# Row maxima of two neighbouring PSUM banks in one VectorE operation, in a transformer kernel with four rotating banks

## The chip, the cores and the metric

The kernel runs on one core of one Trainium2 chip. A core has five engines that run side by side and meet at semaphores: TensorE (PE; its weight loads are a row of their own, PEld), VectorE (DVE), ScalarE (ACT), GpSimd (POOL) and SyncE (SP), which here issues DMAs. The metric is the device time of one launch in microseconds (us). The kernel before takes 1293.03 us, the median of 3 runs (1291.48 to 1293.97).

## What is computed

Two sequences of 1024 tokens with 512 channels go through four residual stages. The first one, causal attention with 32 query heads of 16 channels over a single key/value head and an ALiBi slope per head, is the one that the change touches:

```python
x = x + _layernorm(_L0_attn_ref(_layernorm(x), Wqkv, Wo))      # the stage of the change
x = x + _layernorm(_L0_ffn_ref(_layernorm(x), ...))            # 4-bit weights, 512 -> 1376 -> 512
x = x + _layernorm(_L1_attn_ref(_layernorm(x), ...))           # a masked linear layer
x = x + _layernorm(_L1_ffn_ref(_layernorm(x), ...))            # a linear layer with a Fourier update

# in _L0_attn_ref
scores = jnp.einsum('bqhd,bkd->bhqk', q, k) * scale
scores = jnp.where(causal, scores + slopes * (pos_k - pos_q), NEG_INF)
probs = jax.nn.softmax(scores, axis=-1)
attn = jnp.einsum('bhqk,bkd->bqhd', probs, v).reshape(B, S, H)
return attn @ Wo
```

## The kernel before

Attention goes by 16 blocks of 128 queries (`BLOCKS`: the eight of sequence 0 in rising order, the eight of sequence 1 in falling order). A block is gone through twice.

First pass, `p1` in the code: TensorE computes scores with the queries on the partitions, only to find the maximum of each row. The keys of a block are cut into segments of 512, 256 or 128 (`segments`). One unit ("p1", i, z, h) fills one PSUM bank of 512 columns: one head by 512 keys, two by 256 or four by 128, with a mask matmul added where the segment holds the diagonal (`row_max` in `tensor`, lines 1314 and 1317). VectorE then takes the maxima of that bank with one TENSOR_REDUCE of 512 elements per partition into `mx` (`row_max` in `vector`, line 1125). All blocks together have 576 such banks. When a block has its last unit, `mx` is joined over the segments, turned on TensorE ("mt", line 1364), split into three bf16 parts and sent by DMA into three rows of the block's stacked queries `QS` (line 853).

Second pass: TensorE computes the scores again, now with keys on the partitions and the maximum already subtracted through those rows ("tile", line 1393; mask at 1395) into the three banks of `ST`; ScalarE takes the exponential (line 1048); four tiles make a quad, and TensorE multiplies it with the values ("pv", line 1407, eight records a quad) into the bank `PO`. There are 576 tiles and 144 quads. After a block its sums are turned ("ot", line 1369), divided by the row sums on VectorE (lines 1173 and 1174), turned again ("at", line 1373, split at 1185) and multiplied by Wo ("wo", lines 1379 to 1381).

PSUM has eight banks: three of `ST`, one of `PO` and four of `bank`, the ring (`RING = 4`). Every use of the ring takes the next bank, `AT[u] % RING`: the 576 units of the first pass and 147 other uses (by kind: 32 ot, 20 xt, 20 q, 16 mt, 16 at, 16 wo, 6 dv, 6 ds, 5 kv, 5 vt, 5 dt). TensorE waits before a use until the use four places earlier has been read (`bank_for`), which VectorE or ScalarE tells after reading it.

Every engine runs a fixed program. The order of the work is written by `plan_order`, a list scheduler in Python that runs when the kernel is built. It has a cost for each kind of work (`took` for TensorE; the dictionary in `commit` for the others) and takes in turn what is ready, by a due time. In it a first-pass unit costs TensorE 218 ns plus its mask, and VectorE 690 ns. A unit competes for TensorE with a due time of VectorE's load less 400 ns, tiles with ScalarE's load, other uses of the ring with now plus 500 or 600 ns, and pv with now plus 1500 ns.

Of the kernel before, what the change touches and what calls it, by code (L numbers as in the profile page):

```python
# [15 lines left out]
ALU = mybir.AluOpType  # L16
# [8 lines left out]
P = 128  # L25
# [155 lines left out]

def maxima_of(i):

    return [("p1", i, z, h) for z, (_, w, _) in enumerate(segments(BLOCKS[i][1])) for h in range(0, NH, 512 // w)]


QUAD0 = [0]
# [30 lines left out]
def plan_order():  # L218
# [1 line left out]

    took = {"dt": 400, "dv": 520, "ds": 300, "p1": 218, "tile": 218, "pv": 1060, "xt": 400, "q": 700, "kv": 700, "vt": 400, "mt": 200, "ot": 400, "at": 400, "wo": 700}
    reads = {"pe": 280, "act": 270, "dve": 270, "pool": 200, "sp": 0}
    free = {"pe": 0, "act": 0, "dve": 0, "pool": 0, "sp": 0}
    end, order = {}, {e: [] for e in free}
# [9 lines left out]
    def known(*keys):  # L236
        t = 0
        for k in keys:
            if k not in end:
                return None  # L240
            t = max(t, end[k])
        return t
# [1 line left out]
    def latest(*ts):  # L244
        return None if None in ts else max(ts)

    def bank_ready():
        n = len(bank_of) - RING
        return known(("bank", bank_of[n])) if n >= 0 else 0

    def open_piece(k):
        for t in range(PIECES[k][2]):
# [30 lines left out]

    def pe_choices():
        out = []
        dve_load = free["dve"] + sum(690 for j, r in pend["dve"] if r <= free["pe"] + 300)
        act_load = free["act"] + sum(600 for j, r in pend["act"] if r <= free["pe"] + 300)
        if at["p1"] < len(p1):
            u = p1[at["p1"]]
            i = u[1]  # L290
            deps = [("stacked", i), ("ks", keys_piece(i))]
            if u == maxima_of(i)[0] and i >= 2:
                deps.append(("pe", ("mt", i - 2)))
            out.append((latest(known(*deps), bank_ready()), dve_load - 400, u))
        if at["tile"] < 4 * QUADS:
            n = at["tile"]
            i = BLOCK_OF[n // 4]
            t = known(("max", i), *([("exp", n - ST_RING)] if n >= ST_RING else []))
            out.append((t, act_load, ("tile", n)))
        if at["pv"] < QUADS:  # L300
            q = at["pv"]
            i, a, kb = quad_place(q)
            deps = [("exp", 4 * q + j) for j in range(4)] + [("v", keys_piece(i))]
            if kb == 0 and q:
                deps.append(("evac", q - 1))
            out.append((known(*deps), free["pe"] + 1500, ("pv", q)))
        if turn:
            out.append((latest(end[turn[0][1]], bank_ready()), 0, turn[0][0]))
        for work, late in ((finish_work, 600), (chunk_work, 500)):
            if work:  # L310
                u, need = work[0]
                t = known(need)
                if u[0] not in STEPPED or u[-1] == 0:
                    t = latest(t, bank_ready())
                out.append((t, free["pe"] + late, u))
        return [x for x in out if x[0] is not None]

    def commit_pe(t, u):
        kind = u[0]
        ms = took[kind]  # L320
        if kind == "p1":
            _, w, diag = segments(BLOCKS[u[1]][1])[u[2]]
            ms += 216 * P // w if diag else 0
        if kind == "tile" and diagonal(u[1] // 4):
            ms += 216
        if kind in ("q", "kv") and PIECES[u[1]][2] < 3:
            ms = 720
        e = t + ms
        log.append((t, e, "pe", u))
        end["pe", u] = e  # L330
        free["pe"] = e
        order["pe"].append(u)
        name = u[:-1] if kind in STEPPED else u
        if kind not in ("tile", "pv") and (kind not in STEPPED or u[-1] == 0):
            bank_of.append(name)
        ready = e + reads["pe"]
        if kind == "p1":
            at["p1"] += 1
            pend["dve"].append((u, ready))
            for i, k in ((1, 2), (4, 3), (6, 4), (AFTER_AT, AFTER)):  # L340
                if u == maxima_of(i)[-1]:
                    open_piece(k)
            if u == maxima_of(AFTER_AT)[0]:
                sp_issue(("load", AFTER), e)
                pend["pool"].append((("clear",), e))
                for k in range(CODE_RING):
                    sp_issue(("codes", k), e)
        elif kind == "tile":
            at["tile"] += 1
            pend["act"].append((("exp", u[1]), ready))  # L350
            i = BLOCK_OF[u[1] // 4]
            if u[1] + 1 == TILE_ENDS[i + 1]:
                end["tiles", i] = e
        elif kind == "pv":
            at["pv"] += 1
            end["pv", u[1]] = e
            i, a, kb = quad_place(u[1])
            if kb == BLOCKS[i][1]:
                pend["act"].append((("evac", i, a), ready))
        else:  # L360
            for work in (finish_work, chunk_work, turn):
                if work and work[0][0] == u:
                    work.pop(0)
            if kind in ("xt", "mt", "at", "dt") or (kind in STEPPED and u[-1] == 1):
                pend["act"].append((name, ready))
            if kind in ("vt", "ot"):
                pend["dve"].append((u, ready))
            if kind == "dv":
                pend["act"].append((u, ready))
            if kind == "ds":  # L370
                end["full", u] = ready
                if codes_after(u[1]) is not None:
                    k = codes_after(u[1])
                    sp_issue(("codes", k), max(e, end["q4", k - 2]))
                    pend["dve"].append((("codes", k), max(e, end["codes", k])))
            if kind == "q" and u[-1] == 1:
                sp_issue(("qout", u[1], u[2]), e + 3800)
            if kind == "xt" and u[1] and u[1] + 1 < NC and u[2] == PIECES[u[1]][2] - 1:
                sp_issue(("load", u[1] + 1), e + 2000)
            if kind == "mt":  # L380
                sp_issue(("mdma", u[1]), e + 2300)
                if u[1] + AHEAD < NB:
                    stacks_due.append(u[1] + AHEAD)
        try_stacks()
# [30 lines left out]
    def commit(e, t, j):  # L415
# [38 lines left out]
                pend["dve"].append((j, f + 100))  # L454
        elif e == "dve":
            f = t + {"mx": 200, "mt": 280, "ot": 700, "stats": 900, "mt3": 280, "ys": 1150, "vt": 300, "kv": 750, "norm": 2300, "index": 900, "onehot": 1200,
                     "zeros": 2700, "scales": 1650, "codes": 2600}.get(kind, 690)
            done = f + reads["dve"]
            if kind in ("p1", "xt", "q", "kv", "vt", "mt", "ot", "at", "ds"):
                end["bank", j] = done  # L460
# [113 lines left out]
def uses_in_order():  # L574

    begun, ended = list(FIRST), list(FIRST)
    for u in ORDER["pe"]:
        if u[0] in STEPPED:
            (begun if u[-1] == 0 else ended).append(u[:-1])
        elif u[0] not in ("tile", "pv"):  # L580
            begun.append(u)
            ended.append(u)
    return begun, ended


BEGUN, ENDED = uses_in_order()
AT = {u: n for n, u in enumerate(BEGUN)}
FULL = {u: n + 1 for n, u in enumerate(ENDED)}


# [84 lines left out]
def attention(nc, sem, half_neg, x_dram, wqkv, wo, ident_d, identb_d, mask_d, pos_d, krows_d, gmask_d, x1_dram, ident, identb,  # L675
              wx, xT, xin, QP, qrest, mats, table_loads, dq):
    with ExitStack() as ctx:
# [97 lines left out]
        def at(u):  # L775
            return bank[:, AT[u] % RING, :]

        def full(eng, u):

            eng.wait_ge(bank_full, FULL[u])  # L780
# [23 lines left out]
        def banks_freed(eng, which):  # L804

            for r in which:
                freed(eng, [u for u in BEGUN if AT[u] % RING == r][-1])

        def scores_read(eng):
            eng.wait_ge(p_done, 4 * QUADS)  # L810
# [279 lines left out]
        def vector(v):  # L1090
# [29 lines left out]
            def row_max(u):  # L1120
                _, i, z, h = u
                _, w, _ = segments(BLOCKS[i][1])[z]
                m = 512 // w
                full(v, u)
                v.tensor_reduce(mx[:, i % 2, z, h:h + m], at(u).rearrange("p (m k) -> p m k", m=m), AX.X, ALU.max).then_inc(bank_free_dve, 1)  # L1125

            def join_max(i):
                zs, k = len(segments(BLOCKS[i][1])), i % 2
# [167 lines left out]
        def tensor(pe):  # L1296
            pe.wait_ge(consts_in, 32)

            def bank_for(u):

                if AT[u] >= RING:
                    freed(pe, BEGUN[AT[u] - RING])

            def row_max(u):
                _, i, z, h = u
# [5 lines left out]
                    pe.wait_ge(ks_ready, keys_piece(i) + 1)  # L1311
                bank_for(u)
                for j in range(m):
                    last = pe.matmul(at(u)[:, j * w:(j + 1) * w], QS[0:ROWS1, slot, h + j, :], KS[b][0:ROWS1, k0:k0 + w],  # L1314
                                     start=(j == 0 or not diag), stop=(not diag or w > P), skip_group_check=True)
                if diag:
                    last = pe.matmul(at(u).rearrange("p (m k) -> p m k", m=m)[:, :, w - P:w], identb[:, :],  # L1317
                                     mask[:, 0, 0:m * P].rearrange("p (m k) -> p m k", m=m), start=False, stop=True, skip_group_check=True)
                last.then_inc(bank_full, 1)

            def fill(u, step=None):
# [1001 lines left out]
```

## Time and profile before

| | us |
|---|---|
| median of 3 runs | 1293.03 |
| lowest, highest | 1291.48, 1293.97 |
| the profiled execution | 1289.91 |
| its span, first to last instruction | 1288.1 |
| first pass: first and last row maximum start at | 39.1, 637.9 |
| mean granted TensorE clock | 0.977 of full speed |

The profile is of a single execution. "Busy" is the time that an engine has an instruction in work; matmuls overlap one another, so that a TensorE that is busy need not be at its peak. A wait is told as the idle time of an engine ahead of an instruction, with the instruction that ended it. Since weight loads run under the matmul in front, a wait of PEld need not stop the array, and one of PE does. Some matmul records can be missing from a trace.

### The profile page before, as it was taken

What the parts mean: (1) busy time and instruction counts of PE and PEld (TensorE: products, weight loads), DVE (VectorE), ACT (ScalarE), POOL (GpSimd) and SP (SyncE); (2) the same over time, 40 slices, a digit from 0 to 9 for tenths busy, and PEclk for the clock granted to TensorE, in tenths of its full rate; (3) what the DMA queues carried; (4) which work ended last, traced back from release to release, by engine and by line L of the source; (5) the groups of instructions that cost most, each with busy time, mean ns of one, the idle gap of its engine ahead of it and who ended that gap; (6) DMA issues with size and microseconds to landing.
All of it is one profiled execution on the core that took longest, in us unless ns stands there. A gap on an engine that the chain in (4) does not pass through costs nothing. (4 is left out here: it accounts for less than half of the span.)

```text
span 1288.1 us, 16700 instructions
## 1 busy us (share of the span) xinstructions
PE 1170.8 (91%) x6137; PEld 715.2 (56%) x6208; DVE 715.8 (56%) x1374; ACT 583.2 (45%) x1047; POOL 338.5 (26%) x366
## 2 busy tenths in 40 slices
PE   4879999999989999999998799999999999299995
PEld 4535534543543433344535577788788787256663
DVE  4378598688678897788713643331421300655654
ACT  5425456465547677857574443211111111134443
POOL 1214114112220231211034554111211111115554
PEclk9989999999989999999999999999999999699998
DMA  4451502400140420303120222300200100500304
GB/s 157 97 83 55 94 18 42 108 17 18 29 87 1 107 34 18 75 18 67 28 99 26 73 66 87 107 22 1 98 1 1 66 1 1 150 28 5 126 0 130
DMA packets 71567, 72.15 MB, mean 56 GB/s; under 512 B 39826, under 2 KB 45226, under 8 KB 71468
## 3 DMA queue, kind: packets, MB, share of 16 engines
q1 hardware_dynamic: 67284, 60.35, 18.8%
q0 software_dynamic: 3152, 8.63, 2.1%
q10 hardware_dynamic: 1056, 2.16, 0.5%
q8 instruction: 47, 0.77, 0.2%
q14 instruction: 28, 0.23, 0.1%
HBM read 51.86 MB, written 18.87 MB: 55 GB/s over the span
## 5 line engine op out<-in xcount | busy, mean ns | idle before, releaser
L1125 DVE TENSOR_REDUCE mx<-bank 128x1 f32<-128x512 f32 (+2 forms) x576 | 364.6, 684 | 98.5 <-PE bank L1317 54.7
L1048 ACT ACTIVATE PT<-ST 128x512 f32<-128x512 f32 x576 | 311.4, 600 | 106.4 <-PE ST L1393 62.4
L1314 PE MATMUL bank<-KS,QS 125*128 125x512 bf16 (+2 forms) x896 | 204.1, 309 | 12.5 <-DMA QS<-q_scratch 4.2
L1393 PE MATMUL ST<-QS,KS 128*128 128x512 bf16 x527 | 185.0, 383 | 9.1 <-DMA QS<-mparts 3.3
L1407 PE MATMUL PO<-PT,V 128*32 128x512 f32 x1152 | 152.8, 604 | 1.4 <-ACT PT L1048 1.0
L1694 DVE TENSOR_TENSOR f_h<-f_h,f_pair 128x512 f32<-128x512 f32 (+1 forms) x44 | 30.2, 687 | 207.5 <-ACT f_h L1643 207.5
L1314 PEld LDWEIGHTS bank<-KS,QS 125*128 125x128 bf16 x896 | 78.5, 99 | 113.3 <-DVE mx L1125 33.5
L56 PE MATMUL f_pair<-f_xT,gw 128*128 128x512 f32 (+1 forms) x352 | 140.0, 398 | 0.0
L58 PE MATMUL f_pair<-f_xT,gw 128*128 128x512 f32 (+1 forms) x352 | 137.9, 392 | 0.0
L57 PE MATMUL f_pair<-f_xT,gw 128*128 128x512 f32 (+1 forms) x352 | 137.9, 392 | 0.0
L1643 ACT ACTIVATE f_h<-f_pair 128x512 f32<-128x512 f32 (+1 forms) x44 | 26.3, 598 | 218.9 <-PE f_pair L58 218.8
L1393 PEld LDWEIGHTS ST<-QS,KS 128*128 128x128 bf16 x576 | 51.5, 97 | 125.2 <-ACT PT L1048 76.2
L1607 POOL TENSOR_TENSOR f_h_part<-f_h,f_h_part 128x512 fp32r<-128x512 f32 (+1 forms) x44 | 56.9, 1294 | 228.6 <-ACT f_h_part L1647 228.6
L905 POOL TENSOR_TENSOR yrstd<-ymom,half_neg 128x1 f32<-128x1 f32 x16 | 9.0, 562 | 358.8 <-DVE ymom L1202 358.8
L58 PEld LDWEIGHTS f_pair<-f_xT,gw 128*128 128x128 f32 (+1 forms) x352 | 65.7, 187 | 15.3
L56 PEld LDWEIGHTS f_pair<-f_xT,gw 128*128 128x128 f32 (+1 forms) x352 | 65.6, 186 | 15.0 <-ACT y L1026 0.3
L57 PEld LDWEIGHTS f_pair<-f_xT,gw 128*128 128x128 f32 (+1 forms) x352 | 65.6, 186 | 14.4
L1761 PE MATMUL f_Y<-dw,f_h_part 128*128 128x512 f32 (+1 forms) x176 | 71.3, 405 | 2.1 <-POOL f_h_part L1607 2.1
L1763 PE MATMUL f_Y<-dw,f_h_part 128*128 128x512 f32 (+1 forms) x176 | 68.7, 390 | 0.0
L1762 PE MATMUL f_Y<-dw,f_h_part 128*128 128x512 f32 (+1 forms) x176 | 68.6, 390 | 0.0
L1317 PE MATMUL bank<-mask,identb 128*128 128x128 bf16 (+2 forms) x246 | 67.1, 273 | 0.0
L2150 PE MATMUL l_psum<-l_wT,l_xT 128*128 128x512 f32 x128 | 54.2, 423 | 0.0
(208 smaller groups left out, 1806.6 us busy)
## 6 DMA issues: line engine op xcount, KB each, us to landing
QS<-q_scratch SPq DMA_DIRECT2D x96, 128.0 KB
l_x<-x_dram SPq DMA_DIRECT2D x12, 512.0 KB, 4.1
q_scratch<-QP SPq DMA_DIRECT2D x36, 128.0 KB, 1.9
xres<-_attn_hidden_states_dram POOLq DMA_DIRECT2D x16, 256.0 KB, 3.1
x_dram<-xout POOLq DMA_DIRECT2D x16, 256.0 KB, 2.4
xin<-x_dram SPq DMA_DIRECT2D x4, 1024.0 KB, 7.6
f_xsum<-x_dram SPq DMA_DIRECT2D x4, 1024.0 KB, 7.2
x_dram<-f_xsum SPq DMA_DIRECT2D x4, 1024.0 KB, 4.6
```

The lines of the kernel that those rows point to most:

```text
L56: pe.matmul(out, w_hi(c), x_hi(c), start=(c == 0), stop=False)
L57: pe.matmul(out, w_hi(c), x_lo(c), start=False, stop=False)
L58: last = pe.matmul(out, w_lo(c), x_hi(c), start=False, stop=(c == chunks - 1))
L1048: act.activation(PT[:, quad % PT_RING, n % 4, :], ST[:, n % ST_RING, :], ACT.Exp).then_inc(p_done, 1)
L1125: v.tensor_reduce(mx[:, i % 2, z, h:h + m], at(u).rearrange("p (m k) -> p m k", m=m), AX.X, ALU.max).then_inc(bank_free_dve, 1)
L1314: last = pe.matmul(at(u)[:, j * w:(j + 1) * w], QS[0:ROWS1, slot, h + j, :], KS[b][0:ROWS1, k0:k0 + w], start=(j == 0 or not diag), stop=( ...
L1317: last = pe.matmul(at(u).rearrange("p (m k) -> p m k", m=m)[:, :, w - P:w], identb[:, :], mask[:, 0, 0:m * P].rearrange("p (m k) -> p m k" ...
L1393: last = pe.matmul(dst, KS[b][0:ROWS2, kb * P:(kb + 1) * P], QS[0:ROWS2, slot, h:h + 4, :], start=True, stop=not diag)
L1407: last = pe.matmul(PO[32 * j:32 * (j + 1), :], V[b][:, kb, :], PT[:, q % PT_RING, j, :], start=(kb == 0), stop=(kb == qb))
L1761: pe.matmul(Y[:, t, :], hi(h_parts[0][0:w, s, at]), hi(dw[0:w, 0, n % 2, :]), start=(n == 0), stop=False)
L1762: pe.matmul(Y[:, t, :], hi(h_parts[0][0:w, s, at]), hi(dw[0:w, 1, n % 2, :]), start=False, stop=False)
L1763: last = pe.matmul(Y[:, t, :], hi(h_parts[1][0:w, s, at]), hi(dw[0:w, 0, n % 2, :]), start=False, stop=(n == NT - 1))
```

## The change

A unit of the first pass becomes two neighbouring banks: heads h.. in the first and heads 16 + h.. in the second. TensorE fills both (each matmul and mask is issued for t = 0 and 1), signals once, and VectorE reads both with one TENSOR_REDUCE of 1024 elements per partition. There are 288 units instead of 576. The ring still has four banks, and a pair may start at bank 0, 1 or 2; where it would start at bank 3, that bank is left out once (`skipped`, `take_banks`). A pair waits until both of its banks are free. In the planner a pair costs TensorE 436 ns plus two masks and VectorE 1130 ns.

```diff
 def maxima_of(i):
-    return [("p1", i, z, h) for z, (_, w, _) in enumerate(segments(BLOCKS[i][1])) for h in range(0, NH, 512 // w)]
+    return [("p1", i, z, h) for z, (_, w, _) in enumerate(segments(BLOCKS[i][1])) for h in range(0, NH // 2, 512 // w)]
+
+def banks_of(u):
+    return 2 if u[0] == "p1" else 1
+
+def skipped(n, count):
+    return int(count == 2 and n % RING == RING - 1)
+
+def take_banks(taken, u):
+    if skipped(len(taken), banks_of(u)):
+        taken.append(taken[len(taken) - RING])
+    taken.extend([u] * banks_of(u))
...
-    took = {"dt": 400, "dv": 520, "ds": 300, "p1": 218, "tile": 218, "pv": 1060, ...
+    took = {"dt": 400, "dv": 520, "ds": 300, "p1": 436, "tile": 218, "pv": 1060, ...
...
-    def bank_ready():
-        n = len(bank_of) - RING
-        return known(("bank", bank_of[n])) if n >= 0 else 0
+    def bank_ready(count=1):
+        n = len(bank_of) - RING + skipped(len(bank_of), count)
+        return known(*(("bank", bank_of[x]) for x in range(n, n + count) if x >= 0))
...
-        dve_load = free["dve"] + sum(690 for j, r in pend["dve"] if r <= free["pe"] + 300)
+        dve_load = free["dve"] + sum(1130 if j[0] == "p1" else 690 for j, r in pend["dve"] if r <= free["pe"] + 300)
...
-                     "zeros": 2700, "scales": 1650, "codes": 2600}.get(kind, 690)
+                     "zeros": 2700, "scales": 1650, "codes": 2600, "p1": 1130}.get(kind, 690)
...
+        def both(u):
+            return bank[:, AT[u] % RING:AT[u] % RING + 2, :]
...
             def row_max(u):      # VectorE
                 full(v, u)
-                v.tensor_reduce(mx[:, i % 2, z, h:h + m], at(u).rearrange("p (m k) -> p m k", m=m), AX.X, ALU.max).then_inc(bank_free_dve, 1)
+                v.tensor_reduce(mx[:, i % 2, z, :].rearrange("p (t h) -> p t h", t=2)[:, :, h:h + m], both(u).rearrange("p t (m k) -> p t m k", m=m), AX.X, ALU.max).then_inc(bank_free_dve, 1)
...
             def bank_for(u):
-                if AT[u] >= RING:
-                    freed(pe, BEGUN[AT[u] - RING])
+                for n in range(AT[u], AT[u] + banks_of(u)):
+                    if n >= RING:
+                        freed(pe, BEGUN[n - RING])
...
             def row_max(u):      # TensorE
                 for j in range(m):
-                    last = pe.matmul(at(u)[:, j * w:(j + 1) * w], QS[0:ROWS1, slot, h + j, :], KS[b][0:ROWS1, k0:k0 + w],
-                                     start=(j == 0 or not diag), stop=(not diag or w > P), skip_group_check=True)
+                    for t in range(2):
+                        last = pe.matmul(both(u)[:, t, j * w:(j + 1) * w], QS[0:ROWS1, slot, NH // 2 * t + h + j, :], KS[b][0:ROWS1, k0:k0 + w],
+                                         start=(j == 0 or not diag), stop=(not diag or w > P), skip_group_check=True)
```

## Rows read from the trace of the kernel before

**Rows 1.** The page: the span, and each engine's busy time, share and instructions.

```profile
span 1288.1 us, 16700 instructions
PE 1170.8 (91%) x6137; PEld 715.2 (56%) x6208; DVE 715.8 (56%) x1374; ACT 583.2 (45%) x1047; POOL 338.5 (26%) x366
```

**Rows 2.** Busy time by stretch: PE, PEld, DVE, ACT, POOL; granted clock, DMA share, GB/s.

```profile
39.00:97.00 58.00, 45.55 (x261) 28.44 (x264) 32.85 (x62) 17.53 (x37) 11.11 (x10) 0.94 0.45 90
97.00:380.00 283.00, 264.20 (x1516) 129.73 (x1538) 210.73 (x383) 155.96 (x295) 70.47 (x55) 0.98 0.24 51
380.00:640.00 260.00, 253.34 (x1622) 107.91 (x1649) 220.28 (x405) 182.34 (x349) 47.72 (x52) 1.00 0.21 45
640.00:700.00 60.00, 54.84 (x309) 24.79 (x313) 12.44 (x34) 36.41 (x70) 19.82 (x19) 0.97 0.20 67
700.00:1060.00 360.00, 350.99 (x1593) 279.30 (x1599) 113.23 (x201) 88.32 (x147) 99.17 (x76) 1.00 0.14 47
```

**Rows 3.** The page's costliest groups: count, busy us, mean ns, idle before and its releaser.

```profile
L1125 DVE TENSOR_REDUCE mx<-bank 128x1 f32<-128x512 f32 (+2 forms) x576 | 364.6, 684 | 98.5 <-PE bank L1317 54.7
L1314 PE MATMUL bank<-KS,QS 125*128 125x512 bf16 (+2 forms) x896 | 204.1, 309 | 12.5 <-DMA QS<-q_scratch 4.2
L1393 PE MATMUL ST<-QS,KS 128*128 128x512 bf16 x527 | 185.0, 383 | 9.1 <-DMA QS<-mparts 3.3
L1407 PE MATMUL PO<-PT,V 128*32 128x512 f32 x1152 | 152.8, 604 | 1.4 <-ACT PT L1048 1.0
```

**Rows 4.** Timeline around 307 us, PE alone: two quads' value products, one behind the other.

```profile
306.83 1.07 PE L1407 MATMUL PO<-PT,V 128*32 128x512 f32 x8
...
309.67 1.06 PE L1407 MATMUL PO<-PT,V 128*32 128x512 f32 x8
```

**Rows 5.** Waits of 39 to 700 us: who for whom, total us, times, longest.

```profile
DVE mx L1125 <- PE bank L1317: 54.7, 63, 2.6
DVE mx L1125 <- PE bank L1314: 38.7, 57, 3.4
...
PEld ST L1393 <- ACT PT L1048: 76.2, 105, 1.0
PEld bank L1314 <- DVE mx L1125: 33.5, 56, 1.1
...
PEld bank L1364 <- DVE mx L1125: 4.6, 7, 0.8
```

**Rows 6.** The same view, of PE alone, where the array itself stood.

```profile
PE bank L1373 <- DVE A L1174: 5.0, 6, 2.1
PE bank L1340 <- DVE qrest L1149: 4.1, 4, 1.4
```

**Rows 7.** Groups of VectorE with shapes apart: one of 256 elements, one of 2048.

```profile
L1174 DVE TENSOR_TENSOR A<-bank,rsum 128x256 f32<-128x256 f32 x32 | 13.6, 425 | 1.1
...
L2004 DVE TENSOR_REDUCE l_msum<-early 128x64 f32<-128x2048 int32 x1 | 2.2, 2217 | 0.0
```

**Rows 8.** Timeline of eight row maxima back to back, and TensorE's answers to freed banks.

```profile
79.48 4.87 DVE L1125 TENSOR_REDUCE mx<-bank 128x2 f32<-128x512 f32 x8
...
80.22 0.11 PEld L1314 LDWEIGHTS bank<-KS,QS 125*128 125x128 bf16 x2 [0.83 <-DVE mx L1125]
...
80.81 0.11 PEld L1314 LDWEIGHTS bank<-KS,QS 125*128 125x128 bf16 x2 [0.37 <-DVE mx L1125]
```

**Rows 9.** Timeline at 305 us: one bank filled, and the reduce that waited for it.

```profile
305.21 0.38 PE L1314 MATMUL bank<-KS,QS 125*128 125x512 bf16 x1
...
305.63 2.48 DVE L1125 TENSOR_REDUCE mx<-bank 128x1 f32<-128x512 f32 x4 [0.19 <-PE bank L1314]
```

**Rows 10.** Timeline at the end of a block's first pass, around 189 us.

```profile
188.93 0.09 PEld L1364 LDWEIGHTS bank<-ident,mx 128*32 128x32 f32 x1 [0.28 <-DVE mx L1125]
...
190.13 0.10 PEld L1314 LDWEIGHTS bank<-KS,QS 125*128 125x128 bf16 x1 [0.50 <-DVE mx L1125]
```

**Rows 11.** Busy time by stretch, columns as in rows 2, after a stall of TensorE.

```profile
369.00:372.00 3.00, 2.65 (x7) 1.90 (x8) 2.18 (x5) 0.48 (x2) 0.00 (x0) 0.50 0.03 6
```

More of the change, by code:

```diff
@@ L218, in plan_order @@
 def plan_order():
-    took = {"dt": 400, "dv": 520, "ds": 300, "p1": 218, "tile": 218, "pv": 1060, "xt": 400, "q": 700, "kv": 700, "vt": 400, "mt": 200, "ot": 400, "at": 400, "wo": 700}
+    took = {"dt": 400, "dv": 520, "ds": 300, "p1": 436, "tile": 218, "pv": 1060, "xt": 400, "q": 700, "kv": 700, "vt": 400, "mt": 200, "ot": 400, "at": 400, "wo": 700}
     reads = {"pe": 280, "act": 270, "dve": 270, "pool": 200, "sp": 0}
@@ L293, in pe_choices @@
                 deps.append(("pe", ("mt", i - 2)))
-            out.append((latest(known(*deps), bank_ready()), dve_load - 400, u))
+            out.append((latest(known(*deps), bank_ready(2)), dve_load - 400, u))
         if at["tile"] < 4 * QUADS:
@@ L322, in commit_pe @@
             _, w, diag = segments(BLOCKS[u[1]][1])[u[2]]
-            ms += 216 * P // w if diag else 0
+            ms += 2 * 216 * P // w if diag else 0
         if kind == "tile" and diagonal(u[1] // 4):
@@ L334, in commit_pe @@
         if kind not in ("tile", "pv") and (kind not in STEPPED or u[-1] == 0):
-            bank_of.append(name)
+            take_banks(bank_of, name)
         ready = e + reads["pe"]
@@ L580, in uses_in_order @@
         elif u[0] not in ("tile", "pv"):
-            begun.append(u)
+            take_banks(begun, u)
             ended.append(u)
@@ L586 @@
 BEGUN, ENDED = uses_in_order()
-AT = {u: n for n, u in enumerate(BEGUN)}
+AT = {u: BEGUN.index(u) for u in ENDED}
 FULL = {u: n + 1 for n, u in enumerate(ENDED)}
@@ L806, in banks_freed @@
             for r in which:
-                freed(eng, [u for u in BEGUN if AT[u] % RING == r][-1])
+                freed(eng, [u for n, u in enumerate(BEGUN) if n % RING == r][-1])
         def scores_read(eng):
@@ L1313, in row_max @@
                 for j in range(m):
-                    last = pe.matmul(at(u)[:, j * w:(j + 1) * w], QS[0:ROWS1, slot, h + j, :], KS[b][0:ROWS1, k0:k0 + w],
-                                     start=(j == 0 or not diag), stop=(not diag or w > P), skip_group_check=True)
+                    for t in range(2):
+                        last = pe.matmul(both(u)[:, t, j * w:(j + 1) * w], QS[0:ROWS1, slot, NH // 2 * t + h + j, :], KS[b][0:ROWS1, k0:k0 + w],
+                                         start=(j == 0 or not diag), stop=(not diag or w > P), skip_group_check=True)
                 if diag:
-                    last = pe.matmul(at(u).rearrange("p (m k) -> p m k", m=m)[:, :, w - P:w], identb[:, :],
-                                     mask[:, 0, 0:m * P].rearrange("p (m k) -> p m k", m=m), start=False, stop=True, skip_group_check=True)
+                    for t in range(2):
+                        last = pe.matmul(both(u)[:, t, :].rearrange("p (m k) -> p m k", m=m)[:, :, w - P:w], identb[:, :],
+                                         mask[:, 0, 0:m * P].rearrange("p (m k) -> p m k", m=m), start=False, stop=True, skip_group_check=True)
                 last.then_inc(bank_full, 1)
```

## The prediction

> **What bounds the kernel now.** I read the page first, then the busy times by stretch, the costliest groups, the waits, and the timeline at a few places. The page gives the span of 1288.1 us and TensorE as the busiest engine [rows 1]. By stretch [rows 2]: the first pass lives between 39 and 640 us. There TensorE is busy 264.2 of 283 us and then 253.3 of 260 us, VectorE 210.7 and 220.3 us, so VectorE has 72 + 40 = 112 us of its own idle time and TensorE 19 + 7 = 26 us. After 640 us no row maximum is left, and the 360 us from 700 to 1060 belong to a stage that the change doesn't touch. So at most the 601 us from 39 to 640 can change, and what follows shifts with their end.
>
> Is VectorE's row maximum what TensorE waits for? Mostly it is the other way round. The 576 reduces are 364.6 us busy and had 98.5 us of idle time ahead of them, ended by TensorE [rows 3]: 54.7 + 38.7 us in 120 waits [rows 5]. In the reverse direction the weight loads of first-pass matmuls waited 33.5 us in 56 waits, and that of the turn of the maxima 4.6 us in 7 [rows 5], part of it under matmuls still in flight. In the steady middle two quads' value products start 2.84 us apart [rows 4], and in between TensorE has 1.07 us of values and matmuls of 0.22 us for four tiles and four first-pass banks, 2.8 us in all: it is full. The array itself stands at chains, not at the ring: for the divided sums (5.0 us) and for the query rest (4.1 us) [rows 6]. Bursts in which VectorE does set the pace exist: eight reduces in a row at 79 us, each answered by a weight load as soon as a bank is free [rows 8], and short ones at block ends, as at 189 us [rows 10].
>
> **The change part by part.**
>
> *The reduce itself.* Eight reduces in a row take 4.87 us; (4.87 - 0.684) / 7 = 0.598 us from start to start, so 0.086 us of the 0.684 us overlaps the next one [rows 3, 8]. For 1024 elements no row exists. Slope: 684 ns at 512 elements against 425 at 256 is 1.01 ns an element [rows 3, 7]; a reduce of 2048 elements from SBUF took 2217 ns, 1533 ns over that of 512 for 1536 more, 1.00 ns an element [rows 3, 7]. So a pair takes 684 + 512 x 1.00 to 1.05 = 1.20 to 1.22 us; I take 1.21, and start to start 1.21 - 0.086 = 1.13 us. Bounds: 1.11 us (half of the 2048 reduce) and 1.37 us (two single ones, if the second bank starts afresh). Saved: 2 x 0.598 - 1.13 = 0.066 us a pair, 288 x 0.066 = 19 us of VectorE's time. Nearly all of it lies where VectorE waits for TensorE anyway and becomes idle time. On the path it counts only where TensorE waits for a bank: 56 + 7 waits and a few of other lines, some 70, each shorter by half a pair's saving: 70 x 0.033 = -2.3 us.
>
> The Trainium skill has a larger price for the removed instruction: "VectorE: DVE Perf Modes", section on the TRN2 errata, gives 120 cycles at 0.96 GHz of fixed cost for a read from PSUM, 125 ns. By that the 288 removed ones would be 36 us instead of 19 us of VectorE's time, and the waits would shrink by twice as much, to -4.4 us. The trace disagrees: of its pitch of 598 ns, 512 elements at 1.00 to 1.04 ns leave 65 to 86 ns [rows 8].
>
> *TensorE's work.* The same 896 matmuls and 256 masks, in another order; the semaphore waits for banks stay 576 (two for each of 288), the signals are halved. Nothing on the array. Bounds -1 to +1 us (two weight loads more or less exposed for each burst).
>
> *The ring, two pairs.* In a run of pairs alone: from a free bank to TensorE's weight load is 0.06 us (the reduces end at 79.48 + 0.684 = 80.16 and 0.598 later, the loads start at 80.22 and 80.81) [rows 8]; from the start of a bank's matmul to its reduce 0.42 us [rows 9]; the second matmul adds 0.22. So refill and hand-over take 0.70 us and the reduce 1.21: a round trip of 1.91 us, against 2 x 1.13 = 2.26 us that two pairs give VectorE. It holds, with 0.35 us to spare where four single banks had 4 x 0.598 - (0.06 + 0.42 + 0.68) = 1.2 us. A pair of width 128 has eight matmuls of 0.055 us and two masks of 0.22, some 0.45 us more: 2.36 us, just over. Those are 32 of 288 pairs.
>
> *Single uses among pairs.* A use of one bank shifts the pairs: the next one starts at bank 1 and ends at bank 2, the one behind it would start at bank 3, leaves it out, takes banks 0 and 1, and so waits for the pair straight before it. Then nothing is refilled while VectorE reads, and it stands 0.70 us unless it has other work. Counted on the bank order that the planner writes for the kernel before, with its units joined in twos, 88 of 288 pairs would wait for the pair straight before them. 88 x 0.70 = 62 us of VectorE's time, inside its 112 us of idle time [rows 2]: it is hidden as long as TensorE has tiles and values to do meanwhile, and costs where it has none. That is at block ends, where ot, at, wo and mt stand close together [rows 10]. Bounds 0 to 16 x 0.70 = 11 us (once a block). I take three of them uncovered, +2.1 us, since some six places in the trace show TensorE waiting for reduces in a burst, and the single use itself brings VectorE 0.27 to 0.69 us of work.
>
> *The order of the work.* The planner had VectorE at 690 ns a bank where the trace has 598; now it has 565 against my 566. It believes VectorE freer by 576 x 690 - 288 x 1130 ns = 72 us, and will place the first pass earlier among the rest. What that is worth no row shows. Bounds: 0, and TensorE's whole idle time of 26 us [rows 2]. Nearest to it are the turns of the maxima that wait for the last reduce, 4.6 us [rows 5]; with maxima earlier about half of that goes: -2 us.
>
> *Elsewhere.* What is queued behind a reduce on VectorE (the division, the splits) waits up to 1.21 instead of 0.68 us, which falls on the chains of rows 6; I count it in the 2.1 us above.
>
> Sum: -2.3 + 2.1 - 2 = -2.2 us against the profiled execution of 1289.91, so 1287.7. That execution lies 3.1 us under the median of 1293.03; on the median's scale 1290.8, taken as **1291 us**. This case's own range is 1287 to 1295.
>
> **The rivals.**
>
> *The ring of two pairs serialises (slower).* Mechanism: the third pair of an odd alignment waits for the pair straight before it, at block ends, where TensorE has no tile to do. Price 0.70 us each; once a block is 11.2 us, less the 2.3: +9, 1302 us, range 1296 to 1310. It decides from the fourth uncovered one (2.3 / 0.70 = 3.3). A stall can also halve the clock: after that at 366 us the granted clock was 0.50 for 3 us [rows 11], the lower of its two levels, 1.2 GHz, and the 2.65 us of matmuls there would have taken half. For it: the 88, and the thin 0.35 us. Against: VectorE's large idle time, and that the planner knows the rule and puts other work between.
>
> The Trainium skill speaks for this rival too: "Perfetto Trace Analysis", section on optimizing Scalar/DVE operations, says that an engine which isn't saturated but makes bubbles on others is better served by smaller instructions. VectorE here is 74 to 85% busy, so by that rule joining them costs; by the row of the waits it would cost what the uncovered ones do.
>
> *The new order closes the block ends (faster).* If the denser first pass makes the maxima ready before TensorE runs out of tiles, two fifths of TensorE's 26 us go: -10 us, 1283 us, range 1277 to 1287. For it: the 98.5 us that VectorE waits for TensorE show that it could deliver earlier [rows 3]. Against: TensorE is full in the steady middle [rows 4], and tiles also wait for ScalarE, 76.2 us [rows 5], which stays.
>
> *The joined reduce doesn't save.* If it takes 1.37 us, start to start 1.28, VectorE has 288 x 0.086 = 25 us more, 70 waits grow by 0.043 (+3 us), and the round trip of 2.07 us leaves little: with the 2.1 and half of the order's gain 1297 us, range 1294 to 1301. Against it: the slope of rows 3 and 7.
>
> **How the numbers follow.** Forecast 0.45, serialising ring 0.29, order 0.21, no saving 0.05. A change of under 0.2% (2.6 us) can't be told from none. The forecast's case lies across that border: 0.20 faster, 0.23 same, 0.02 slower. With the rivals: faster 0.41, same 0.23, slower 0.36. The range has to reach into both rivals: 1279 to 1304 us leaves out a third of the slower case's chance and a little of the faster one's, and covers the bounds that the order's unknown term makes likely.
>
> **What would show it.** The reduce: 288 of them at a mean of 1.20 to 1.22 us, back to back 1.13; a mean of 1.3 or more proves the price wrong. The ring: waits of PEld at the first-pass matmuls for `mx`, now 33.5 us; well above 45 us, with PE itself standing too, is the serialising case. VectorE's idle time ahead of reduces, now 98.5 us, should grow, by the 19 us saved and by the serialised pairs. The order: the last reduce, now at 637.9 us, starts some 2 us earlier, and in the faster case by 10. TensorE's idle time from 97 to 640 us stays near 26 us in my case. The forecast is wrong if that idle time moves by more than 5 us either way, or if the work after the last reduce, 640 to 700 us, changes its length.

## The result

The changed kernel takes 1299.3 us (median of 8 runs, 1297.1 to 1302.2) against 1292.6 us (8 runs): ratio 1.0050, interval 1.0036 to 1.0064. It is 6.7 us slower. The forecast was 1291 us, faster; the range of 1279 to 1304 us holds the time, the direction is wrong, and the time is near the 1302 us of the slower rival. The profiled execution took 1297.26 us.

The page of the changed kernel: span, busy time by engine, and the groups that answer to rows 3 (count, busy us, mean ns, idle before).

```profile
span 1295.5 us, 16703 instructions
...
PE 1170.6 (90%) x6138; PEld 716.7 (55%) x6208; DVE 699.0 (54%) x1086; ACT 584.7 (45%) x1047; POOL 338.1 (26%) x366
...
L1146 DVE TENSOR_REDUCE mx<-bank 128x2 f32<-128x1024 f32 (+2 forms) x288 | 344.0, 1222 | 103.9 <-PE bank L1337 51.4
...
L1337 PE MATMUL bank<-KS,QS 125*128 125x512 bf16 (+2 forms) x896 | 178.5, 313 | 20.9 <-DVE mx L1146 11.8
L1417 PE MATMUL ST<-QS,KS 128*128 128x512 bf16 x525 | 173.1, 385 | 10.2 <-DMA QS<-mparts 6.0
L1431 PE MATMUL PO<-PT,V 128*32 128x512 f32 x1152 | 153.0, 604 | 2.7 <-ACT PT L1069 2.1
```

VectorE did get its saving: 699.0 us busy instead of 715.8 [rows 1]. But what ends the idle time of the first-pass matmuls is no longer a DMA (4.2 us) but VectorE's reduce, with 11.8 us, and that idle time rose from 12.5 to 20.9 us [rows 3]. The same by stretch, columns as in rows 2:

```profile
39.00:97.00 58.00, 45.89 (x256) 29.16 (x259) 33.31 (x45) 17.16 (x36) 11.39 (x10) 0.88 0.45 90
97.00:380.00 283.00, 258.49 (x1493) 127.50 (x1514) 198.05 (x245) 152.12 (x288) 67.13 (x52) 0.97 0.22 49
380.00:640.00 260.00, 251.71 (x1585) 104.86 (x1614) 207.74 (x263) 183.38 (x347) 51.31 (x54) 1.00 0.23 48
640.00:700.00 60.00, 58.21 (x362) 27.67 (x365) 18.55 (x38) 40.62 (x79) 15.25 (x15) 1.00 0.19 63
```

From 97 to 640 us TensorE is busy 510.2 us instead of 517.5 [rows 2]: 7.3 us more idle time. Over the whole span its idle time grew by 7.6 us (1295.5 - 1170.6 against 1288.1 - 1170.8), about the 7.4 us by which the span grew. TensorE and ScalarE do less between 97 and 640 us, since the same work ends later; VectorE's busy time there falls by 25.2 us, with the saving of the reduces in it, and GpSimd's stays the same. The last reduce starts 12.4 us later (650.3 against 637.9 us), and what follows it is 5 us shorter, so a part of the delay is made up after the first pass. The waits of 39 to 720 us, of TensorE's array itself (compare rows 6, where 5.0 us for the divided sums was the longest):

```profile
PE bank L1337 <- DVE mx L1146: 11.8, 15, 1.6
PE ST L1417 <- DMA QS<-mparts: 6.0, 5, 2.6
PE bank L1397 <- DVE A L1195: 4.2, 2, 2.1
```

In the kernel before, the same view has for the first-pass matmuls:

```profile
PE bank L1314 <- DVE mx L1125: 3.6, 14, 0.6
```

So as many waits (15 and 14), but 8.2 us longer, and the longest 1.6 us instead of 0.6. One of these places, the timeline at 194 us, a block end like that of rows 10:

```profile
192.89 1.23 DVE L1146 TENSOR_REDUCE mx<-bank 128x2 f32<-128x1024 f32 x1 [0.26 <-PE bank L1388]
...
194.26 0.59 PE L1337 MATMUL bank<-KS,QS 125*128 125x512 bf16 x2 [1.55 <-DVE mx L1146]
...
194.85 0.67 DVE L1129 BATCH_NORM_STATS2 stats<-xin 128x6 f32<-128x512 f32 x1
...
194.88 0.72 PE L1397 MATMUL bank<-ident,A 128*128 128x128 f32 x4
...
195.77 1.23 DVE L1146 TENSOR_REDUCE mx<-bank 128x2 f32<-128x1024 f32 x1
...
197.12 0.14 PEld L1337 LDWEIGHTS bank<-KS,QS 125*128 125x128 bf16 x2 [1.85 <-DVE mx L1146]
197.15 1.01 PE L1337 MATMUL bank<-KS,QS 125*128 125x512 bf16 x2 [1.55 <-DVE mx L1146]
```

TensorE stands 1.55 us with its array empty until the reduce that began at 192.89 has ended at 194.12, fills one pair, turns the divided sums (0.72 us), and stands 1.55 us again for the next reduce (195.77 + 1.23 = 197.00). The pair was full at 194.85, but VectorE, which had no second pair ready, had by then gone on to the work that its fixed program puts next (0.67 us of statistics), so the reduce of the new pair began 0.9 us late. The granted clock of the stretch 194 to 199 us is 0.63:

```profile
194.00:199.00 5.00, 2.32 (x8) 0.68 (x8) 4.83 (x13) 0.91 (x2) 0.11 (x1) 0.63 0.03 7
```

In the bank order of the changed kernel 57 of 288 pairs wait for the pair straight before them, and 17 banks are left out. Matched one by one with the reduces of the trace, VectorE idles 0.74 us on average ahead of those 57 and 0.27 us ahead of the other 231. Matched in the same way, 10 of the array's 15 waits for reduces, 9.2 of the 11.8 us, stand ahead of the matmuls of those 57 pairs.

### The profile page after: what moved, and what is told of

Same layout as the page of the kernel before. It is cut to its first block and busy times, and to the rows that moved or that the text cites. A ratio compares the mean times of both kernels' runs of the same rounds, so it can differ in the third digit from the quotient of the medians.

```text
span 1295.5 us, 16703 instructions
## 1 busy us (share of the span) xinstructions
PE 1170.6 (90%) x6138; PEld 716.7 (55%) x6208; DVE 699.0 (54%) x1086; ACT 584.7 (45%) x1047; POOL 338.1 (26%) x366
## 5 line engine op out<-in xcount | busy, mean ns | idle before, releaser
L1146 DVE TENSOR_REDUCE mx<-bank 128x2 f32<-128x1024 f32 (+2 forms) x288 | 344.0, 1222 | 103.9 <-PE bank L1337 51.4
L1337 PE MATMUL bank<-KS,QS 125*128 125x512 bf16 (+2 forms) x896 | 178.5, 313 | 20.9 <-DVE mx L1146 11.8
L1417 PE MATMUL ST<-QS,KS 128*128 128x512 bf16 x525 | 173.1, 385 | 10.2 <-DMA QS<-mparts 6.0
L1337 PEld LDWEIGHTS bank<-KS,QS 125*128 125x128 bf16 x896 | 70.6, 100 | 146.3 <-issue 61.5
L2174 PE MATMUL l_psum<-l_wT,l_xT 128*128 128x512 f32 x128 | 54.3, 424 | 0.0
L2175 PE MATMUL l_psum<-l_wT,l_xT 128*128 128x512 f32 x128 | 51.0, 399 | 0.0
```

The source lines that it names most:

```text
L1146: v.tensor_reduce(mx[:, i % 2, z, :].rearrange("p (t h) -> p t h", t=2)[:, :, h:h + m], both(u).rearrange("p t (m k) -> p t m k", m=m), AX ...
L1337: last = pe.matmul(both(u)[:, t, j * w:(j + 1) * w], QS[0:ROWS1, slot, NH // 2 * t + h + j, :], KS[b][0:ROWS1, k0:k0 + w], start=(j == 0 o ...
L1417: last = pe.matmul(dst, KS[b][0:ROWS2, kb * P:(kb + 1) * P], QS[0:ROWS2, slot, h:h + 4, :], start=True, stop=not diag)
```

## The experiments

Times are medians; ratios are to the kernel before, run on the same chip with each of four batches (1291.7 us with e1 to e4, 1292.0 with e5 to e8, 1292.2 with e9 to e14 but e13, 1290.5 with e13 and e15 to e17). The changed kernel was run apart, beside 1292.6 us. So a difference between two kernels is told below as the difference of their ratios times 1292 us; each ratio's interval is some 0.15 to 0.2% wide to either side, 2 to 3 us, so that a difference of two is good to some 3 to 4 us.

| | kernel | us | ratio (interval) |
|---|---|---|---|
| | changed | 1299.3 | 1.0050 (1.0036 to 1.0064) |
| e1 | changed, no bank left out (planner too) | 1290.2 | 0.9989 (0.9973 to 1.0004) |
| e2 | before, price of a maximum 565 | 1286.0 | 0.9955 (0.9938 to 0.9973) |
| e3 | changed, two reduces a pair | 1303.7 | 1.0088 (1.0065 to 1.0111) |
| e4 | changed's order, old ring | 1293.0 | 1.0014 (0.9999 to 1.0029) |
| e5 | changed's order, none left out at run time | 1299.6 | 1.0060 (1.0038 to 1.0082) |
| e6 | e2, f32 steps 1400 | 1280.9 | 0.9916 (0.9893 to 0.9939) |
| e7 | before, ring of three | 1324.2 | 1.0247 (1.0218 to 1.0276) |
| e8 | e1, filled bank by bank | 1294.3 | 1.0017 (1.0001 to 1.0032) |
| e9 | e5, filled bank by bank | 1298.8 | 1.0050 (1.0033 to 1.0068) |
| e10 | e4, both banks waited for | 1299.7 | 1.0060 (1.0040 to 1.0079) |
| e12 | changed, f32 steps 1400 | 1292.0 | 0.9991 (0.9976 to 1.0007) |
| e13 | e12, no bank left out | 1284.2 | 0.9951 (0.9933 to 0.9969) |
| e14 | before, f32 steps 1400 | 1295.3 | 1.0023 (1.0009 to 1.0037) |
| e15 | e6, price 600 | 1281.1 | 0.9929 (0.9911 to 0.9948) |
| e16 | e12's order, old ring | 1283.2 | 0.9946 (0.9927 to 0.9965) |
| e17 | changed, price of a pair 1380 | 1319.7 | 1.0233 (1.0212 to 1.0254) |

Theory A says that the ring which holds two pairs costs the time, at run time. Theory B says that the order which the planner now writes costs it. A third question is what the joined reduce itself does.

### The order kept, the ring put back: e4

The order stays that of the changed kernel; before the programs are written, each pair is split again.

```diff
+for _e in ("pe", "dve"):
+    ORDER[_e] = [x for u in ORDER[_e] for x in ([u, (*u[:3], NH // 2 + u[3])] if u[0] == "p1" else [u])]
+
+def banks_of(u):
+    return 1
```

> The changed kernel's planned order on every engine, but at run time the old ring: the two banks of a pair are filled, waited for, read (reduces of 512) and freed one by one, and no bank is left out. Theory A (the waits of the ring of two pairs at run time cost the 6.7 us): back to 1290 to 1295 us. Theory B (the order that the planner writes for pairs costs them, the run-time waits don't): stays at 1297 to 1301 us.

Ratio 1.0014 against 1.0050: the old handling of the banks brings back 0.0036 x 1292 = 4.7 us (2.0 to 7.4) in the changed kernel's own order. The order by itself is left with +1.8 us, 0 to 3.7. The wait of the array says the same, 4.5 us in e4 against 11.8:

```profile
PE bank L1348 <- DVE mx L1158: 4.5, 9, 1.2
```

Two other readings can be set against this. The weight loads' waits for reduces don't follow the time: they are 73.1 us in e4 and 45.0 in the changed kernel, which is slower. The granted clock doesn't separate the two either: its mean over the executions is 0.970 in e4 and 0.971 in the changed kernel. It may have a part in the order's +1.8 us: the kernel before has 0.975 on average beside e4, and its own executions there at 0.970 take 1295.4 to 1295.6 us, some 4 us above its median. How much of the 1.8 us that is no run shows.

### The joined reduce undone alone: e3

```diff
-                v.tensor_reduce(mx[...], both(u)..., AX.X, ALU.max).then_inc(bank_free_dve, 1)
+                for t in range(2):
+                    ins = v.tensor_reduce(mx[:, i % 2, z, NH // 2 * t + h:NH // 2 * t + h + m], both(u)[:, t, :].rearrange("p (m k) -> p m k", m=m), AX.X, ALU.max)
+                ins.then_inc(bank_free_dve, 1)
```

> The changed kernel, same order, same ring of two pairs, same waits; only the joined reduce of 1024 elements is undone: two reduces of 512, the second one tells that both banks are free. A pair then keeps VectorE 2 x 0.598 = 1.196 us instead of 1.142, and its release comes 0.06 us later. Theory A (the joined operation saves little, the ring costs): 1300 to 1304 us, +1 to +4 us against the changed kernel. If the joined operation itself were harmful (it holds both banks longer, or its read is slow): faster than the changed kernel's 1299.3 us.

Ratio 1.0088: 4.9 us over the changed kernel and 9.6 us over e4, whose order it shares. So in this order the joined operation gains 4.9 us, and the handling of pairs that it needs (one wait, one fill and one release for two banks) loses 9.6. The array's wait for reduces differs by nearly the same, 13.7 us against e4's 4.5:

```profile
PE bank L1339 <- DVE mx L1147: 13.7, 19, 1.7
```

### Which part of the pair: e5, e9, e10

e5 has the changed kernel's order, but a pair at bank 3 goes on in bank 0.

```diff
+        def part(u, t):
+            return bank[:, (AT[u] + t) % RING, :]
...
+                if AT[u] % RING < RING - 1:
+                    v.tensor_reduce(out, both(u).rearrange("p t (m k) -> p t m k", m=m), AX.X, ALU.max).then_inc(bank_free_dve, 1)
+                else:
+                    for t in range(2):
+                        ins = v.tensor_reduce(out[:, t, :], part(u, t).rearrange("p (m k) -> p m k", m=m), AX.X, ALU.max)
+                    ins.then_inc(bank_free_dve, 1)
```

> The changed kernel's planned order, pairs and joined reduces kept, but at run time no bank is left out: a pair that would start at bank 3 takes banks 3 and 0 (that pair alone read by two reduces of 512). Between the changed kernel (1299.3) and its order on the old ring (1293.0) this splits the 6.3 us. If the left-out banks (17 of them) cost them: 1292 to 1295 us. If it is that two banks are waited for and freed together: 1297 to 1300 us. Half and half: 1295 to 1297 us.

Ratio 1.0060, no less than the changed kernel's 1.0050: leaving a bank out costs nothing measurable at run time in this order. It still has 55 pairs that wait for the pair straight before them (57 in the changed kernel). What costs, by e4, is that two banks go as one.

Next, two kernels with one half of the pairing each. e9 is e5 with the joint release alone: TensorE waits for and fills the first bank, then the second, and one reduce still frees both. e10 is e4 with the joint wait: TensorE waits for both banks ahead of the first, and each bank is read and freed by itself.

```diff
                 for t in range(2):
+                    if AT[u] + t >= RING:
+                        freed(pe, BEGUN[AT[u] + t - RING])
```

> e5 (changed kernel's order, pairs, no bank left out at run time, 1299.6 us) with TensorE waiting for and filling the two banks one after the other; the joined reduce still frees both together. Against the same order on the old ring (e4, 1293.0 us) 6.6 us are to be split into what the joint wait ahead of the fill costs and what the joint release costs. If the joint wait: 1293 to 1296 us. If the joint release (a pair's first bank comes free one half reduce late): 1298 to 1301 us.

```diff
+                if u[3] < NH // 2:
+                    bank_for(u)
+                    bank_for((*u[:3], NH // 2 + u[3]))
...
-                full(v, u)
+                full(v, (*u[:3], NH // 2 + u[3] % (NH // 2)))
```

> The counterpart on e4 (1293.0 us): TensorE waits for both banks before it fills the first, and VectorE begins when both are full, but it reads them with two reduces of 512 and frees each one at once. If the joint wait costs: 1297 to 1300 us. If the joint release costs: 1292 to 1295 us.

Ratios 1.0050 and 1.0060, 4.7 and 5.9 us over e4. By its expectation e9 says that the joint release costs, and by its own e10 says that the joint wait does, so the cost doesn't sit at one end. Each is to be held against the kernel with the whole pairing that reads the banks as it does: e9, with the joined read, is 1.3 us under e5; e10, with two reads, is 3.6 us under e3; neither difference is clear of noise. So either half alone brings most of the cost, and the other half adds no more than these few us. The likely reason, not shown: a bank freed early helps nobody who waits for two, and a wait that ends early helps nobody whose two banks are freed together. What both have, and e4 has not, is also a reader that begins only when both banks are full; a kernel in which VectorE begins on the first bank and all else stays joined wasn't tried, so that this alone costs the time isn't ruled out.

### How much the depth of the ring is worth: e7

```diff
-RING = 4
+RING = 3
```

> The kernel before, single banks and reduces and its own prices, with a ring of three banks instead of four (the fourth is not used); the planner knows it. A measure of what the ring's depth is worth. In the changed kernel a single use between two pairs leaves only three of the four banks in use at best. Theory A (depth of the ring is what is short): slower by more than the change, 1299 to 1315 us. If depth hardly matters (TensorE is full and banks are free when it comes): 1291 to 1296 us, and theory A' (the left-out bank's direct wait on the pair before) alone stays.

1324.2 us, ratio 1.0247, +32 us, more than expected. The ring's fourth bank, with the order planned anew for three, is worth 2.5% to a kernel whose TensorE is 93 and 97% busy [rows 2]. Two pairs in four banks are a loss of depth each time that a single use stands between pairs; how much of e7's loss that brings e7 doesn't say.

### The price alone, and pairs at the old price: e2, e17

```diff
-        dve_load = free["dve"] + sum(690 for j, r in pend["dve"] if r <= free["pe"] + 300)
+        dve_load = free["dve"] + sum(565 if j[0] == "p1" else 690 for j, r in pend["dve"] if r <= free["pe"] + 300)
...
-                     "zeros": 2700, "scales": 1650, "codes": 2600}.get(kind, 690)
+                     "zeros": 2700, "scales": 1650, "codes": 2600, "p1": 565}.get(kind, 690)
```

> The kernel before, single banks and single reduces, with only the planner's price of a row maximum on VectorE lowered from 690 to 565 ns a bank, which is what the change's 1130 ns a pair says. It measures the order term of the prediction by itself. Prediction's term: -2 us (0 to -10), so 1283 to 1293 us, likeliest 1291. Theory B (the denser order is what makes the change slower): 1297 to 1301 us.

1286.0 us, -5.8 us: a denser order is not what makes the change slower, and theory B in this form falls; of the order that is planned for pairs, e4 leaves +1.8 us. Telling the planner what the change tells it, and changing nothing else, is a gain, between my term of -2 and the faster rival's -10 us. The changed kernel holds a gain from the price too, as e17 shows (the two places above at 1380 a pair instead of 1130):

> The changed kernel with the planner's price of a pair on VectorE at 1380 ns, twice the 690 ns of a single bank before; everything else as changed. If the change is -5.8 us by the truer price and about +12.5 us by the pairs: some 1305 us (1302 to 1309). If the price did nothing in the changed kernel: 1297 to 1301 us.

Ratio 1.0233, 24 us over the changed kernel; some 6 were expected, and the sum of the two parts doesn't hold. In its own order 37 banks instead of 17 are left out, 78 pairs instead of 57 wait for the pair straight before them, and the array waits 27.1 us for reduces:

```profile
PE bank L1337 <- DVE mx L1146: 27.1, 30, 2.1
```

Pairs at the old price cost 30 us; the truer price saves 24 us with pairs and 5.8 without. Why so much more with pairs is argued, not shown: the planner sees VectorE nearly full and the ring standing at once.

### No bank left out, known to the planner: e1, e8

e1 has e5's diff and `skipped` that returns 0 for the planner too.

> The changed kernel without the rule that leaves a bank out: a pair may start at bank 3 and then takes banks 3 and 0 (such a pair alone is read by two reduces of 512, 0.06 us more). The planner knows it. 17 left-out banks go; of pairs that wait for the pair straight before them there are 64 of 288 instead of 57. Theory A (a ring that holds two pairs is too short, the left-out bank is a detail): the loss of 6.7 us against the kernel before stays mostly, 1296 to 1301 us. Theory A' (the left-out bank is the cost): back to 1291 to 1295 us. Theory B (the planner's new order is worse by chance): anything, since the order changes again.

1290.2 us, ratio 0.9989, 7.9 us less than the changed kernel, though 64 pairs wait for the pair before them. Since e5 shows that the left-out banks cost nothing while the order stands, the 7.9 us come with the new order: the planner no longer plans around them, or that order is a lucky one. Its order on the old ring wasn't run. e8 is e1 with the wait of e9.

> e1 (pairs without left-out banks, 1290.2 us, same order), but TensorE waits for the first bank of a pair, fills it, and only then waits for the second; the joined reduce stays. 64 pairs wait for the pair straight before them in one of their banks, and where only the second bank is the late one the first is filled under the reduce. Theory A: some 10 to 30 fills of 0.22 us come earlier, -1 to -4 us, 1286 to 1290 us. If waiting for both banks at once costs nothing: 1289 to 1292 us.

1294.3 us, ratio 1.0017, 3.6 us slower than e1 instead of 1 to 4 us faster. The order is the same, and no wait is longer by the program's text; the intervals of the two overlap by a hair. The granted clock goes with a part of it: its mean is 0.968 in e8 and 0.971 in e1, and the executions at 0.969 lie closer, 1292.0 to 1294.8 us in e8 and 1292.1 to 1292.6 in e1. Why e8 isn't faster stays open.

### Another order: e12, e16, e13, and the planner's other price

The planner also had a step of six f32 matmuls at 700 ns, where the trace has 0.23 us from start to start, 1.4 us a step.

```diff
-    took = {..., "q": 700, "kv": 700, ..., "wo": 700}
+    took = {..., "q": 1400, "kv": 1400, ..., "wo": 1400}
```

> The kernel before with the price of a row maximum at 565 ns (as e2, 1286.0 us) and the planner's price for a step of six f32 matmuls (q, kv, wo) at 1400 ns instead of 700; the trace has 0.23 us a matmul, 1.4 us a step. Tests whether truer prices go on helping. If e2's 5.8 us come from a truer plan: 1278 to 1286 us. If they are the luck of one order: anything from 1284 to 1296 us.

> The changed kernel, with the planner's price of a step of six f32 matmuls put from 700 to 1400 ns. Its counterpart with single banks is e6 (1280.9 us, price of a row maximum 565 ns). Tests whether the pairs lose as much in another, better order. If the ring of pairs is the cause: slower than e6 by some 6 us, 1284 to 1292 us. If the loss belongs to one order: 1279 to 1283 us.

> e12's planned order (pairs, f32 steps at 1400 ns; 1292.0 us) on the old ring: each bank waited for, read and freed by itself. The repeat of e4 in another order. If the handling of pairs at run time is what costs: 1284 to 1288 us, some 6 us less than e12. If that was peculiar to the first order: 1290 to 1294 us.

> e12 with no bank left out (as e1), planner told. If the left-out banks make the planner's orders worse, as e1 against the changed kernel suggests (-9 us): 1280 to 1287 us. If e1 was the luck of an order: 1288 to 1296 us.

> The kernel before with the price of the f32 steps at 1400 ns alone, the row maximum still at 690 ns. With e2 (the other price alone, 1286.0 us) and e6 (both, 1280.9 us) it says whether the two corrections add up or whether one is luck. Adding up: 1285 to 1289 us (about -5). No effect of its own: 1291 to 1294 us.

> e6 (single banks, f32 steps 1400 ns) with the row maximum at 600 ns, the pitch of the trace, instead of 565. If truer prices are what helps: 1278 to 1284 us, as e6. If e6 is the luck of one order: 1284 to 1296 us.

e6 with single banks has a ratio of 0.9916 and e12 with pairs 0.9991: the pairs lose 9.7 us here. e16 keeps e12's order and handles the banks one by one: 0.9946, 5.8 us less. That repeats e4's 4.7 us in a second order. The array's wait for reduces falls with it; e12, then e16:

```profile
PE bank L1337 <- DVE mx L1146: 7.7, 13, 1.5
```

```profile
PE bank L1348 <- DVE mx L1158: 3.3, 9, 0.9
```

e13 is 5.2 us under e12, as e1 was 7.9 us under the changed kernel: that the planner need not leave banks out helped twice, which speaks against luck. With it the pairs lose little of what they cost: e1 is level with the kernel before, and e13 with e16, though not with e6. e14 is 3.0 us slower than before: the truer price of the f32 steps alone doesn't help, and together with a truer maximum it does (e6 against e2, -5.0 us). Orders thus move the time by a few us either way, and a single comparison of two proves little. e15, at the pitch of the trace, is level with e6. e6 and e15 are the fastest kernels here, 0.8 and 0.7% under the kernel before, with single banks.

## Why the prediction was wrong

**The price of the reduce: right.** 1.21 us was predicted, 1.222 is the mean of the 288 (1.202 to 1.228); two back to back take 2.36 us, so 2.36 - 1.22 = 1.14 us from start to start, against 1.13:

```profile
81.50 2.36 DVE L1146 TENSOR_REDUCE mx<-bank 128x4 f32<-128x1024 f32 x2
```

The second bank costs no fresh start: 538 ns for 512 more elements. The rival that the joined reduce doesn't save is out.

**The gain of the reduce: mis-sized.** -2.3 us was the term, 70 waits by half a pair's saving; e3 measures -4.9 us. In a ring of pairs a wait is for the whole pair, so it is shortened by the whole saving and not by half; that would double the term, to -4.6 us, but no run shows the waits one by one.

**Single uses among pairs: the step that failed.** The mechanism was named, with 0.70 us a pair and a count; the term was set to three uncovered ones, +2.1 us, where e3 against e4 measures +9.6 us for the handling of pairs as a whole. No run separates the pairs that wait for the one straight before them from the rest, but the trace of the changed kernel puts most of it there: 10 uncovered ones, 9.2 us, against the 3.6 us that the array waited for reduces in the kernel before. I held VectorE's 112 us of idle time [rows 2] to be cover. It is no cover: what has to be hidden is TensorE's standing, and at block ends it has no tile to do. The price was too low as well, since 0.70 us is VectorE's standing. TensorE's lasts as long as the reduce and what the program has put ahead of it: 0.92 us on average in those 10 places, and 1.55 us twice in a row at 194 us. The reading in front of it, that the array stands at chains and not at the ring, was too strong: the third row of that view is the ring's, 3.6 us in 14 waits. The sign of the whole followed from this term: 9.6 - 4.9 = +4.7 us, e4 against the changed kernel.

**The order: no gain, since only half of it was seen.** -2 us was the term. The lower price alone is worth -5.8 us (e2). But the planner now also plans round pairs and left-out banks, and the sum, measured on the old ring, is +1.8 us, 0 to 3.7 (e4); with +4.7 us for the pairs it makes the 6.5 us of the ratio 1.0050. I had no row for it and named none of its own costs.

**The rival that came true** was the serialising ring, 1302 us with a chance of 0.29. Its sum was near by luck in part: 11.2 - 2.3 = +8.9 us from 16 places at 0.70 us, where the runs have 9.6 - 4.9 and 1.8 us of order, +6.5. Its signs were right in part. The array's waits for first-pass reduces went from 3.6 to 11.8 us, and TensorE's idle time from 97 to 640 us rose by 7.3 us, over the 5 us at which the forecast was to be wrong. But PEld's waits there were to go well above 45 us and are 45.0, and e4, which is faster, has 73.1: they don't tell the case. The last reduce was to start 2 us earlier and starts 12.4 us later. VectorE's idle time ahead of reduces was to grow by 19 us or more and rose only from 98.5 to 103.9 us. Its whole idle time from 97 to 640 us did grow by 25 us, from 112 to 137: the rest of it stands ahead of its other work.

The rule of the Trainium skill ("Perfetto Trace Analysis", section on optimizing Scalar/DVE operations) that smaller instructions serve an engine that isn't saturated but makes others wait holds here for the handling as a whole: e4 against the changed kernel. For the instruction alone it doesn't: e3, with smaller reduces and the same waits, is slower. Nor is an earlier release enough: e10 frees each bank at once, still waits for both, and is no faster than the changed kernel. What helps is that wait, fill, read and release all go by the single bank.

## What to carry to other kernels

Joining two buffers of a ring for the sake of one larger instruction saves a fixed cost on the reading engine and takes freedom from the ring; with four buffers the freedom was worth more (9.6 against 4.9 us). Count the places at which the writer has nothing else to do, not the idle time of the reader. And when a change to a planned kernel also changes the planner's prices, measure the prices alone: here they were a gain that the change hid (e2), and truer prices with the old ring gave the fastest kernels. A rule that the planner must keep has a price too: without the left-out banks the pairs came out level with the kernel before (e1).

## What the runs showed of the hardware

A TENSOR_REDUCE over two neighbouring PSUM banks runs through the bank's edge without a stop that the trace shows: 684 ns for one bank, 1222 ns for two, 1.05 ns for each further element. Its overlap with the next one is the same 0.08 us. A ring of three PSUM banks instead of four, with the order planned anew, cost this kernel 32 us, where 7 to 23 were expected.
